# Reordered engine queues, an earlier coefficient load and shifted filter copies in a four-layer convolution kernel

## The chip, the cores and the metric

The kernel runs on one core of one Trainium2 chip. A core has TensorE (matmul, shown as PE, its weight loads as PEld), VectorE (DVE), ScalarE (ACT), GpSimd (POOL) and SyncE (SP), the last used here only to issue transfers, and 16 DMA engines. The metric is the device time of one execution in microseconds (us).

## The reference

The input x has 8 images of 64 channels of 256 x 256 float32. Four layers follow each other:

```python
# layer 0: attention over channels
att = einsum('bcn,bdn->bcd', q, q); att = softmax(max(att) - att)
x = gamma * einsum('bcd,bdn->bcn', att, q) + x
# layers 1 and 3: a separable long convolution per channel, k = hx (x) hy, causal in both axes
y = irfft2(rfft2(x, s=512) * rfft2(k, s=512) / 512, s=512)[..., :256, :256] + x * bias
# layer 2: shrinkage between a 2-D Haar transform and its inverse, two terms
f1 = haar2d(x)
for i in range(2):
    f4 = einsum('bchw,oc->bohw', f1 * v[i], conv_w[i])
    acc += sign(f4) * relu(abs(f4) - tau[i])
x = haar2d(acc, inverse=True) + x
```

hx and hy come from a small network of sines; they are computed once, at the start.

## The kernel before

Convolutions are done as products with Toeplitz matrices (`toeplitz`, four matmuls of 256 and 128 columns), the Haar transforms as products with sign matrices (`haar_fwd`, `haar_halves`, `haar_inv`). A Toeplitz matrix is never stored: a table of 128 partitions x 256 columns holds, in partition p, the filter from element p on, and it is loaded from `filt` in DRAM by `window` (line 228), which reads 128 overlapping rows of 1 KB, each one float further. Each (image, channel) plane needs two such tables (`tab_a`, `tab_b`, four buffers each) per convolution.

The work of the 8 images is software-pipelined in `timeline` (line 102). A forward stage `forward_stage(b, fwd, shrink, gram)` walks over 64 steps, four to a loop round (`quads`, line 68). In one step it does up to three things, for three different images of the batch: fwd is layer 1 and the forward Haar transform of one channel plane of image b+1, in five lagged parts (`on[0]` to `on[4]`); shrink is the middle of layer 2 for image b, 4 x 256 pixels of all channels per step, in halves a = 0 and 1; gram is a piece of layer 0's Gram matrix of image b+2. An inverse stage then does the inverse Haar transform and layer 3 of image b (inv) and layer 0's mixing of image b+2 (mix). There are one mixing-only start, one forward stage without shrinkage (b=-1), six forward stages with all three parts (b=0 to 5), one without Gram (b=6), one with shrinkage alone (b=7), and the inverse stages between them.

Every engine has its queue written out by hand, in program order, and waits on semaphores. The order inside one full step is, before the change:

- SP (line 288): wait for x1 and the second Toeplitz product of four planes back, load image (256 KB) and two tables (128 KB each); in odd j then wait for a turn (`c_copy`) and load 512 KB of coefficients, then 512 KB of pixels for the Gram.
- PE (line 486): first Toeplitz product of plane n (bank 0); product(0) of the shrinkage (line 498, bank 4); half a Gram piece; second Toeplitz product of plane n-1 (bank 1); product(1) (bank 5); the other half of the Gram piece; Haar (line 441); halves (line 457); turn (line 509), four transposes that wait for DVE's field of the step before.
- ACT (line 637): store of finished coefficients (line 659, an issue on its queue, waits for DVE's row repair); mid (664), the copy of bank 0; Abs(0) (643), Sign(0) (647), Relu(0) (652); Abs(1), Sign(1); high part of a plane (674); Relu(1); res (683).
- DVE (line 816): scale(0) (828), which reads product(0); two repairs of one row (843, 844); less(0) (835); field of the step before (853), which needs POOL's pair sums; scale(1); x1 (862); less(1); low part (869).
- POOL (line 932): for a = 0, 1 the multiplication by the sign (937) and the pair sum (940).

A product may overwrite its bank when the Relu of the same half of the step before is done (`c_relu`).

## Time and profile before

| | us |
|---|---|
| median of 3 runs | 7283.22 (7279.34 to 7286.21) |
| profiled execution | 7309.31 |
| its span | 7307.5 |
| PE busy in it | 6528.9 (89%) |
| PE weight loads | 5505.1 (75%) |
| DVE busy | 4081.2 (56%) |
| ACT busy | 3933.3 (54%) |
| POOL busy | 2583.9 (35%) |

The span runs from the first to the last instruction of the profiled execution; busy shares are averages over stages with different limits, so the stages are read one by one. A bracket behind an instruction says how long its engine stood idle before it and what ended that.

### The profile page before, as it was taken

The numbers are of one execution on the slowest core, as the hardware profiler recorded it, in microseconds if no ns is written. First come the engines' busy times: TensorE is split into PE (matmuls) and PEld (weight loads), VectorE is DVE, ScalarE is ACT, GpSimd is POOL, SyncE is SP. The second block draws the span as 40 slices with busy tenths as digits, with TensorE's granted clock in tenths as the row PEclk, the third lists the DMA queues.
The fourth block names the chain that finished last, engine by engine and source line by source line (L and its number), as shares of the span: only waits on it lengthen the run. The fifth ranks groups of instructions, "written<-read, shape, count | busy, mean of one in ns | idle before, by whom it ended". The sixth has DMA issues, their size and how long they took to land.

```text
span 7307.5 us, 143896 instructions
## 1 busy us (share of the span) xinstructions
PE 6528.9 (89%) x37984; PEld 5505.1 (75%) x37984; DVE 4081.2 (56%) x7293; ACT 3933.3 (54%) x7193; POOL 2583.9 (35%) x2564
## 2 busy tenths in 40 slices
PE   6896898999989999999999999899999988897679
PEld 4593787888878787787877888788887877686469
DVE  1241566556654566555664466645665466665556
ACT  1232565555655565555655566555655556655655
POOL 0000444224432344324442244423443244434642
PEclk9898999999999999999999999999999999999889
DMA  6786665876658666686667766586666855554136
GB/s 199 214 214 218 160 166 151 211 187 165 160 152 235 166 161 163 170 222 159 165 156 198 196 161 167 144 236 172 163 160 168 228 139 132 130 116 95 45 74 130
DMA packets 768925, 1214.59 MB, mean 166 GB/s; under 512 B 78742, under 2 KB 473143, under 8 KB 768664
## 3 DMA queue, kind: packets, MB, share of 16 engines
q1 hardware_dynamic: 621208, 942.99, 55.0%
q10 hardware_dynamic: 147456, 268.50, 9.6%
q8 instruction: 117, 1.92, 0.1%
q14 instruction: 144, 1.18, 0.1%
HBM read 808.13 MB, written 403.05 MB: 166 GB/s over the span
## 4 chain that ended last, share of the span: by engine, by line
PE 52%; DVE 11%; DMA 11%; issue 9%; ACT 8%; ACTq 3%; POOL 2%; SPq 2%; DVEq 1%; POOLq 0%
PE ps L431 17%; PE ps L433 9%; PE ps L449 7%; PE ps L498 6%; DMA rows<-coef 5%; PE ps L575 5%; PE ps L457 4%; DVE held L828 4%; ACT ps L643 3%; DMA mixed<-x 3%; DVE field L853 3%; ACT sgn L647 3%; PE ps L509 3%; ACTq L659 2%; DVE res L844 2%
## 5 line engine op out<-in xcount | busy, mean ns | idle before, releaser
L937 POOL TENSOR_TENSOR mag<-mag,sgn 128x512 f32<-128x512 f32 x1024 | 1187.9, 1160 | 2774.9 <-ACT mag L652 2772.9
L952 POOL TENSOR_TENSOR split_a<-field,split_a 128x512 fp32r<-128x512 f32 x512 | 652.1, 1274 | 1810.7 <-ACT split_a L712 1810.7
L835 DVE TENSOR_TENSOR ps<-ps,tau_t 128x512 f32<-128x512 f32 x1024 | 716.5, 700 | 1009.4 <-ACT ps L643 966.5
L431 PE MATMUL ps<-tab_a,img 128*128 128x256 f32 x4096 | 1244.6, 386 | 27.1 <-issue 11.0
L431 PE MATMUL ps<-tab_b,mid 128*128 128x256 f32 x4096 | 1229.3, 382 | 1.6 <-DVE x L862 1.5
L828 DVE TENSOR_TENSOR held<-ps,v_t 128x512 f32<-128x512 f32 x1024 | 704.3, 688 | 409.3 <-PE ps L498 380.0
L664 ACT ACTIVATE mid<-ps 128x512 f32<-128x512 f32 x512 | 305.7, 597 | 1154.4 <-PE ps L433 931.3
L433 PEld LDWEIGHTS ps<-tab_a,img 128*128 128x128 f32 x4096 | 785.1, 192 | 109.2
L433 PEld LDWEIGHTS ps<-tab_b,mid 128*128 128x128 f32 x4096 | 781.7, 191 | 106.7
L643 ACT ACTIVATE ps<-held 128x512 f32<-128x512 f32 x1024 | 613.8, 599 | 426.8 <-DVE held L828 426.8
L433 PE MATMUL ps<-tab_a,img 128*128 128x128 f32 x4096 | 792.2, 275 | 0.0
L433 PE MATMUL ps<-tab_b,mid 128*128 128x128 f32 x4096 | 789.8, 275 | 0.0
L940 POOL TENSOR_TENSOR pair_sum<-mag 128x256 f32<-128x256 f32 x1024 | 743.9, 727 | 121.9 <-POOL mag L937 81.2
L449 PE MATMUL ps<-s_inv,split_a 128*128 128x256 f32 x4096 | 701.7, 315 | 72.3 <-POOL split_a L952 39.1
L431 PEld LDWEIGHTS ps<-tab_a,img 128*128 128x128 f32 x4096 | 669.0, 193 | 102.9 <-issue 51.9
L449 PEld LDWEIGHTS ps<-s_inv,split_a 128*128 128x128 f32 x4096 | 551.0, 194 | 227.9 <-issue 213.3
L652 ACT ACTIVATE mag<-ps 128x512 f32<-128x512 f32 x1024 | 607.4, 593 | 177.9 <-DVE ps L835 177.9
L409 PEld LDWEIGHTS ps<-pix 128*128 128x128 f32 x4096 | 592.6, 192 | 89.9 <-DMA pix<-in_x_pix 48.8
L409 PE MATMUL ps<-pix 128*128 128x128 f32 x4096 | 613.9, 277 | 42.0 <-DMA pix<-in_x_pix 42.0
L431 PEld LDWEIGHTS ps<-tab_b,mid 128*128 128x128 f32 x4096 | 629.4, 193 | 6.2 <-DVE x L862 2.1
L700 ACT ACTIVATE x<-ps 128x512 f32<-128x512 f32 x512 | 306.2, 598 | 606.9 <-DMA mixed<-x 330.2
L647 ACT ACTIVATE sgn<-held 128x512 bf16<-128x512 f32 x1024 | 630.8, 616 | 0.0
(74 smaller groups left out, 10026.9 us busy)
## 6 DMA issues: line engine op xcount, KB each, us to landing
pix<-in_x_pix SPq DMA_DIRECT2D x256, 512.0 KB, 7.0
mixed<-x ACTq DMA_DIRECT2D x512, 256.0 KB, 5.3
img<-mixed SPq DMA_DIRECT2D x512, 256.0 KB, 2.8
tab_a<-filt SPq DMA_DIRECT2D x1024, 128.0 KB, 3.7
tab_b<-filt SPq DMA_DIRECT2D x1024, 128.0 KB, 4.7
coef<-res ACTq DMA_DIRECT2D x512, 256.0 KB, 3.9
out<-res SPq DMA_DIRECT2D x512, 256.0 KB, 4.8
pix<-in_x_rows SPq DMA_DIRECT2D x128, 512.0 KB, 6.0
```

The source lines that it names most:

```text
L409: mm = nc.tensor.matmul(ps[:, 7, 0:2 * C], pix[:, buf, j, :], pix[:, buf, j, :], start=False, stop=False, skip_group_check=True)
L431: nc.tensor.matmul(o_ps, src[:, 0, H * half:H * half + H], tab[:, N - 1::-1], start=True, stop=False)
L433: mm = nc.tensor.matmul(o_ps[:, H:N], src[:, 1, H * half:H * half + H], tab[:, N - 1:H - 1:-1], start=False, stop=True)
L449: mm = nc.tensor.matmul(ps[:, bank, N * half:N * half + N], src[:, piece, kh, H * half:H * half + H], s_inv[:, kh, :], start=(kh == 0 and ...
L643: nc.scalar.activation(ps[:, 4 + a, :], held[:, a], ACT.Abs).then_inc(c_abs, 1)
L647: nc.scalar.activation(sgn[:, a], held[:, a], ACT.Sign).then_inc(c_sign, 1)
L652: nc.scalar.activation(mag[:, a], ps[:, 4 + a, :], ACT.Relu).then_inc(c_relu, 1)
L828: nc.vector.tensor_tensor(held[:, a].rearrange(grouped, i=2, h=4), ps[:, 4 + a, :].rearrange(grouped, i=2, h=4), table(v_t, a), ALU.mult)\
L835: nc.vector.tensor_tensor(bank, bank, table(tau_t, a), ALU.subtract).then_inc(c_less, 1)
L937: nc.gpsimd.tensor_tensor(mag[:, a], mag[:, a], sgn[:, a], ALU.mult).then_inc(c_mult, 1)
L940: nc.gpsimd.tensor_tensor(pair_sum[:, a], mag[:, a, 0:N], mag[:, a, N:2 * N], ALU.add)\
L952: nc.gpsimd.tensor_tensor(split_a[:, 1], src, split_a[:, 0].bitcast(F32), ALU.subtract)\
```

## The change

It changes the order of the queues in the forward stages, and the way in which the filters lie in DRAM:

- PE: product(0), first Toeplitz product, product(1), half Gram, second Toeplitz product, half Gram, and the rest as before. The wait of the first step for the last result of the inverse stage (`i_res`) goes with product(0) to the front.
- ACT: mid; Abs(0), Sign(0), Abs(1), Sign(1), Relu(0); the store of coefficients; high part; Relu(1); res.
- DVE: scale(0); row repairs; scale(1); less(0); field; less(1); x1; low part.
- SP: in odd j the wait for the turn and the load of coefficients stand ahead of the wait for x1 and of the loads of image and tables. The load of pixels stays behind them.
- `filt` holds eight copies of each filter, copy s starting s floats further, with a pitch of 376 floats (1504 bytes). Eight stores write them. `window` reads partition 8a+s from copy s at offset 8a; each read still is 128 rows of 1 KB.

```diff
--- before.py
+++ after.py
@@ -33,6 +33,8 @@
 EMB = 33
 ORDER = 64
 QROW = N + H
+SHIFTS = 8
+SROW = QROW - SHIFTS
 CR = 5
 ROWS = 4
 CHUNKS = N // (2 * ROWS)
@@ -125,7 +127,7 @@
         def sem(name):
             return ctx.enter_context(nc.semaphore(name))
 
-        filt = nc.dram_tensor("filt", (4, C, QROW), F32, kind="Internal").ap()
+        filt = nc.dram_tensor("filt", (4, C, SHIFTS, SROW), F32, kind="Internal").ap()
         coef = nc.dram_tensor("coef", (B, C, H, 2 * N), F32, kind="Internal").ap()
         mixed = nc.dram_tensor("mixed", (C, H, 2 * N), F32, kind="Internal").ap()
 
@@ -227,8 +229,8 @@
 
         def window(f, c):
 
-            row = filt[f, bass.ds(c, 1), :]
-            return bass.AP(row.tensor, row.offset, [[1, H], [1, N]])
+            row = filt[f, bass.ds(c, 1), :, :]
+            return bass.AP(row.tensor, row.offset, [[SHIFTS, H // SHIFTS], [SROW, SHIFTS], [1, N]])
 
 
         @block.sync
@@ -278,7 +280,9 @@
                     load_pix(0, 2 * jj + buf, buf)
             sp.wait_ge(dve_init, 100)
             sp.nop(nofuse=True)
-            sp.dma_start(filt.rearrange("f c n -> c f n"), f_out).then_inc(filters_out, 16)
+            for s in range(SHIFTS):
+                sp.dma_start(filt[:, :, s, :].rearrange("f c n -> c f n"), f_out[:, :, s:s + SROW])\
+                    .then_inc(filters_out, 16)
 
             def forward_stage(b, fwd, shrink, gram):
                 if gram:
@@ -287,6 +291,10 @@
 
                 def step(q, j, on):
                     n = 64 * (b + 1) + 4 * q + j
+                    if shrink and j % 2 and not (isinstance(q, int) and q == 0):
+                        sp.wait_ge(c_copy, 64 * b + 4 * q + j - 3 + CR)
+                        sp.nop(nofuse=True)
+                        load_coef(b, 2 * q + j // 2, j // 2)
                     if fwd and not (isinstance(q, int) and q == 0):
                         sp.wait_ge(f_x1, n - 3 + CR)
                         sp.nop(nofuse=True)
@@ -295,10 +303,6 @@
                         load_img(4 * q + j, j)
                         fwd_tables(4 * q + j, j)
                     if j % 2 and not (isinstance(q, int) and q == 0):
-                        if shrink:
-                            sp.wait_ge(c_copy, 64 * b + 4 * q + j - 3 + CR)
-                            sp.nop(nofuse=True)
-                            load_coef(b, 2 * q + j // 2, j // 2)
                         if gram:
                             load_pix(b + 2, 2 * q + j // 2, j // 2)
                 quads(sp, 16, 0, step)
@@ -371,7 +375,7 @@
                         sp.wait_ge(s, 16 * (32 * (b + 2) + 32) + 16)
                         sp.nop(nofuse=True)
                     if b == -2:
-                        sp.wait_ge(filters_out, 16)
+                        sp.wait_ge(filters_out, 16 * SHIFTS)
                         sp.nop(nofuse=True)
                     else:
                         sp.wait_ge(f_mm2, 64 + CR)
@@ -516,16 +520,18 @@
                         if e % 2 and second:
                             mm.then_inc(gram_chunk, 1)
 
+                    if shrink and on[0]:
+                        if isinstance(q, int) and q == 0 and j == 0:
+                            pe.wait_ge(i_res, 64 * b + CR)
+                            pe.nop(nofuse=True)
+                        product(0)
                     if fwd and on[0]:
                         pe.wait_ge(img_in[j], 16 * (16 * (b + 1) + q) + 16)
                         pe.wait_ge(ftab_in[j], 32 * (16 * (b + 1) + q) + 32)
                         pe.wait_ge(f_mid, n + CR)
                         toeplitz(0, img[:, j], tab_a[:, j]).then_inc(f_mm1, 1)
                     if shrink and on[0]:
-                        if isinstance(q, int) and q == 0 and j == 0:
-                            pe.wait_ge(i_res, 64 * b + CR)
-                            pe.nop(nofuse=True)
-                        product(0)
+                        product(1)
                     if gram and on[1]:
                         gram_half(0)
                     if fwd and on[1]:
@@ -533,8 +539,6 @@
                         pe.wait_ge(f_mid, n + CR)
                         pe.wait_ge(f_x1, n - 1 + CR)
                         toeplitz(1, mid[:, d1 % 2], tab_b[:, d1 % 4]).then_inc(f_mm2, 1)
-                    if shrink and on[0]:
-                        product(1)
                     if gram and on[1]:
                         gram_half(1)
                     if fwd and on[2]:
@@ -651,6 +655,16 @@
                         act.wait_ge(c_pair, u + a - 1 + CR)
                         nc.scalar.activation(mag[:, a], ps[:, 4 + a, :], ACT.Relu).then_inc(c_relu, 1)
 
+                    if fwd and on[0]:
+                        act.wait_ge(f_mm1, n + 1 + CR)
+                        act.wait_ge(f_mm2, n - 1 + CR)
+                        nc.scalar.activation(mid[:, j % 2], halved(ps[:, 0, :]), ACT.Copy).then_inc(f_mid, 1)
+                    if shrink and on[0]:
+                        absolute(0)
+                        sign(0)
+                        absolute(1)
+                        sign(1)
+                        relu(0)
                     if fwd and on[4]:
                         d = j - 4
                         act.wait_ge(f_res, n - 4 + 1 + CR)
@@ -658,16 +672,6 @@
                         dst = coef[bass.ds(b + 1, 1), bass.ds(4 * q + d, 1), :, :].rearrange("b o p n -> p (b o n)")
                         act.dma_start(dst, res[:, d % 2].rearrange("p a n -> p (a n)"))\
                             .then_inc(coef_out[d % 2], 16)
-                    if fwd and on[0]:
-                        act.wait_ge(f_mm1, n + 1 + CR)
-                        act.wait_ge(f_mm2, n - 1 + CR)
-                        nc.scalar.activation(mid[:, j % 2], halved(ps[:, 0, :]), ACT.Copy).then_inc(f_mid, 1)
-                    if shrink and on[0]:
-                        absolute(0)
-                        sign(0)
-                        relu(0)
-                        absolute(1)
-                        sign(1)
                     if fwd and on[2]:
                         act.wait_ge(f_mm3, n - 1 + CR)
                         act.wait_ge(f_mm4, n - 2 + CR)
@@ -843,6 +847,7 @@
                         nc.vector.tensor_tensor(mean, mean, ps[0:1, 3, N:2 * N], ALU.add)
                         nc.vector.tensor_tensor(detail, ps[0:1, 3, 0:N], detail, ALU.subtract).then_inc(f_res, 1)
                     if shrink and on[0]:
+                        scale(1)
                         less(0)
                     if shrink and on[1]:
                         d = j - 1
@@ -854,7 +859,7 @@
                                                 ps[:, 6, :].rearrange("p (a c h) -> p a c h", a=2, h=4),
                                                 ALU.add).then_inc(c_field, 1)
                     if shrink and on[0]:
-                        scale(1)
+                        less(1)
                     if fwd and on[1]:
                         d = j - 1
                         dve.wait_ge(f_mm2, n + CR)
@@ -862,8 +867,6 @@
                         nc.vector.scalar_tensor_tensor(out=x1[:, d % 2], in0=img[:, d % 4],
                                                        scalar=bias1[:, bass.ds(4 * q + d, 1)], in1=halved(ps[:, 1, :]),
                                                        op0=ALU.mult, op1=ALU.add).then_inc(f_x1, 1)
-                    if shrink and on[0]:
-                        less(1)
                     if fwd and on[2]:
                         dve.wait_ge(f_hi, n - 1 + CR)
                         nc.vector.tensor_tensor(split_b[:, 1], halved(ps[:, 2, :]), split_b[:, 0].bitcast(F32),
```

## Rows read from the trace of the kernel before

**Rows 1.** Equal stretches: PE, PEld, DVE, ACT, POOL busy (x count), clock, DMA share, GB/s.
```profile
340.00:580.00 240.00, 240.00 (x1679) 225.57 (x1678) 103.51 (x199) 82.49 (x147) 0.00 (x0) 1.00 0.80 208
2480.00:2960.00 480.00, 443.99 (x2758) 386.54 (x2757) 314.51 (x536) 288.07 (x537) 226.47 (x240) 1.00 0.64 162
5920.00:6380.00 460.00, 377.76 (x2236) 324.72 (x2235) 309.94 (x529) 285.33 (x531) 220.86 (x235) 1.00 0.53 133
6690.00:7020.00 330.00, 202.38 (x693) 133.90 (x693) 189.79 (x288) 200.25 (x345) 216.67 (x231) 0.81 0.17 48
2130.00:2430.00 300.00, 297.30 (x1662) 246.07 (x1662) 154.20 (x306) 166.36 (x304) 76.23 (x60) 0.99 0.78 204
```

**Rows 2.** Line 509 in stages b=2, 6, 7: duration ns, first to last start.
```profile
L509 PE MATMUL ps<-eye,split_a x128: 272/273/330, 2461.5 to 2954.8; 128*128 128x128 f32 x128
...
L509 PE MATMUL ps<-eye,rows x128: 272/273/330, 2481.0 to 2970.6; 128*128 128x128 f32 x128
...
L509 PE MATMUL ps<-eye,split_a x128: 272/273/330, 5897.1 to 6369.7; 128*128 128x128 f32 x128
...
L509 PE MATMUL ps<-eye,rows x128: 271/273/330, 5909.0 to 6385.2; 128*128 128x128 f32 x128
...
L509 PE MATMUL ps<-eye,split_a x128: 272/328/477, 6669.2 to 7019.4; 128*128 128x128 f32 x128
...
L509 PE MATMUL ps<-eye,rows x128: 272/330/477, 6681.3 to 7031.0; 128*128 128x128 f32 x128
```

**Rows 3.** Line 441 in the forward-only stage, the same view.
```profile
L441 PEld LDWEIGHTS ps<-s_fwd,x x400: 188/192/192, 341.7 to 579.9; 128*128 128x128 f32 x134
```

**Rows 4.** Timeline of one step, PE alone: start, duration, what.
```profile
2607.91 0.66 PE L509 MATMUL ps<-eye,rows 128*128 128x128 f32 x4 [0.51 <-DVE field L853]
...
2608.40 0.60 PE L431 MATMUL ps<-tab_a,img 128*128 128x256 f32 x2
...
2609.71 1.03 PE L498 MATMUL ps<-chan_w,rows 128*128 128x256 f32 x4
...
2610.57 0.61 PE L409 MATMUL ps<-pix 128*128 128x128 f32 x4
...
2611.02 0.60 PE L431 MATMUL ps<-tab_b,mid 128*128 128x256 f32 x2
...
2614.45 0.71 PE L457 MATMUL ps<-split_b,s_fwd_half 128*128 128x512 f32 x2
...
2615.66 0.66 PE L509 MATMUL ps<-eye,rows 128*128 128x128 f32 x4 [0.49 <-DVE field L853]
```

**Rows 5.** Timeline of the same step, DVE and ACT.
```profile
2610.97 0.69 DVE L828 TENSOR_TENSOR held<-ps,v_t 128x512 f32<-128x512 f32 x1
...
2611.58 0.40 DVE L843 TENSOR_TENSOR res<-res,ps 1x256 f32<-1x256 f32 x1
...
2611.90 0.41 DVE L844 TENSOR_TENSOR res<-ps,res 1x256 f32<-1x256 f32 x1
...
2612.59 0.34 ACTq L659 DMA_DIRECT2D coef<-res  x1
...
2613.60 0.60 ACT L643 ACTIVATE ps<-held 128x512 f32<-128x512 f32 x1
...
2614.92 0.68 DVE L853 TENSOR_TENSOR field<-pair_sum,ps 128x512 f32 x1
```

**Rows 6.** Timeline of a late coefficient load.
```profile
2627.08 0.33 SPq L266 DMA_DIRECT2D rows<-coef  x1
...
2633.90 1.13 PE L498 MATMUL ps<-chan_w,rows 128*128 128x256 f32 x4 [0.34 <-DMA rows<-coef]
```

**Rows 7.** DMA issues in an inverse part (2130 to 2430): KB, median us to landing.
```profile
tab_b<-filt SPq DMA_DIRECT2D x57, 128.0 KB, 5.1
```

**Rows 8.** The page: a costly group, and the filter store among the DMA issues.
```profile
L937 POOL TENSOR_TENSOR mag<-mag,sgn 128x512 f32<-128x512 f32 x1024 | 1187.9, 1160 | 2774.9 <-ACT mag L652 2772.9
...
filt<-field SPq DMA_DIRECT2D x1, 384.0 KB, 4.6
```

## The prediction

> **What bounds the kernel now.** I read four views. First the busy times in equal stretches, one per kind of stage. They show that TensorE is the busiest engine everywhere, but not equally: in the forward part without shrinkage (340 to 580 us) it is busy for all of 240.0 us, in an inverse part 297.3 of 300 us, in shrinkage with forward part and Gram 444.0 of 480 us, without Gram 377.8 of 460 us, and in shrinkage alone 202.4 of 330 us [rows 1]. So the stages that the diff touches are the ones in which TensorE waits.
>
> Second, the turns of line 509, one group of four per step, which give the length of a step. The 64 steps of stage b=2 run from 2461.5 to 2970.6 us: 8.07 us a step. The six stages with Gram lie at 7.96 to 8.07, mean 8.03; the one without Gram takes 487.7/63 = 7.74, shrinkage alone 361.4/63 = 5.73 [rows 2].
>
> Third, the timeline of TensorE over one step: from 2608.40 (first Toeplitz product) to 2614.45 everything is back to back, then TensorE stands for 0.49 us until the turn at 2615.66, and the row says for whom: DVE's field of line 853 [rows 4]. Turn to turn this step is 7.75 us.
>
> Fourth, the other engines in that step [rows 5]: product(0) starts at 2609.71 only because the first Toeplitz product stands ahead of it; scale(0) follows at 2610.97, the two row repairs at 2611.58 and 2611.90, ACT's store of the coefficients (queued ahead of mid, and waiting for that repair) at 2612.59, then mid, Abs at 2613.60, less(0), field at 2614.92, turn, and again the Toeplitz product. That ring closes in 7.75 us. It is latency through four engines, no engine's own work. On top of it every other step is longer: the coefficient load is issued at 2627.08, behind an image and two tables, and product(0) starts at 2633.90, released by that DMA [rows 6]. The mean of 8.03 over the ring's 7.75 is this lateness, 0.28 us a step.
>
> **The change part by part.** *TensorE's own need per step.* The nearest proof of what it can do back to back is the forward-only stage: 50 steps, 8 loads each, from 341.7 to 579.9 us, so about (238.2 - 0.8)/49 = 4.85 us for two Toeplitz products, Gram, Haar and halves, with no wait [rows 1, 3]. Two products cost 0.86 each (2609.71 to 2610.57) and the turn 0.49 (2607.91 to 2608.40) [rows 4], counted as 0.45 when the next work is already there. Floor: 4.85 + 1.72 + 0.45 = 7.02, taken as 7.05. Nothing is removed from TensorE; the change can give at most the 0.98 us between 8.03 and 7.05.
>
> *Does the new order reach the floor?* I lay one step out, TensorE without waits, product(0) at 0: Toeplitz 0.86, product(1) 2.17, Gram 3.03, Toeplitz 3.48, Gram 4.79, Haar 5.24, halves 6.1, turn 6.55, next product(0) 7.0. A product is read 1.26 us after its start (2609.71 to 2610.97), and successors on one engine start 0.5 (ACT) and 0.6 us (DVE) apart [rows 4, 5]. DVE: scale(0) 1.26, repairs 1.86 and 2.2, scale(1) 3.43, less(0) 4.03, field 4.64, less(1) 5.25, x1 5.9, low part 7.7, done 8.4. ACT: mid 2.6, Abs 3.1, Sign 3.6, Abs 4.15, Sign 4.7, Relu(0) 5.2, store 5.8 to 6.5, high part 7.0 (it needs the halves of the image before, 6.1 + 0.9), Relu(1) 7.5, res 8.0, done 8.6. POOL, from Relu(0)'s end at 5.8: multiply 1.16 [rows 8] and pair sum about 0.75, then those of Relu(1) from 8.2 to about 10.2. Each of TensorE's waits then has room: the next product(0), at 7.0, needs Relu(0), done at 5.8; product(1), at 9.2, needs Relu(1), 8.1; the next turn, at 13.55, needs field, 12.3, which needs the pair sums of 10.2 and starts at 11.6. The least room is 1.0 us. ACT's store, until now in the ring, hides behind these; if that cover went, its 0.7 us would delay Relu(1), which has 1.0. The next thing late is TensorE itself.
>
> *Coefficients asked for earlier.* On SP's queue the load of step (q, j) is now ahead of that step's wait for x1 and of its image and two tables, so it goes out right behind the former trio, one step (7 us) and 2 us of issues sooner. Its own wait (turn of step 4q+j-4) is then already met, so nothing is queued behind it for long; the image and tables behind it have buffers four deep and about 15 us of room. Needed 12 us after its issue where 6.8 us pass in [rows 6], the 0.28 goes. With the new engine order but the old place it would be late by about 1 us in every second step. The pixel load of the Gram stays behind the tables.
>
> *Stages with Gram:* 0.98 x 63 x 6 = 370 us. *Without Gram:* the floor is less by the two Gram halves, 0.45 each (2610.57 to 2611.02 [rows 4]), 6.15; the same layout leaves ACT 0.5 us and the turn 0.3 us of room, I take 6.25: (7.74 - 6.25) x 63 = 94 us. *Shrinkage alone:* here POOL's two multiplies and pair sums, Relu(1) and the next product(1) form a ring over two steps, some 9.9 us; I take 5.1: 0.63 x 63 = 40 us, with ends 0 and 60, since the granted clock is 0.81 there [rows 1], part of the time on the 1.2 GHz level.
>
> *What it costs.* At each entry the first Toeplitz product now stands behind product(0) and its waits for i_res and the coefficients: no row shows this order; between 0 and two products on the 1.2 GHz level (3.4 us) each, I take 1.5 x 7 = 10 us. The filter store becomes eight: 384 KB landed in 4.6 us [rows 8]; eight such, 37 us if serial, 5 if only the issues count, and the first x_rows loads stand behind them on the same queue; I take 10 us, once.
>
> *Tables in copies.* Same bytes, same 128 rows of 1 KB, another address pattern in HBM. In an inverse stage tab_b lands in 5.1 us [rows 7] and TensorE is busy 99% [rows 1], so a faster table is hidden: 0 to -3 us a stage, I take -10 in all. DMA share is 0.64 in the stages with Gram; in 7.05 instead of 8.0 us a step it becomes about 0.73, and the forward-only stage ran at 0.80 without one wait of TensorE [rows 1].
>
> The rows thus say that a 1 KB table row is cheap to hide whatever its start. The Trainium skill ("DMA: Bandwidth & Descriptors", How a descriptor splits into AXI transactions) speaks against this part: a transaction must start at a 256 B boundary, and bytes in front of an unaligned start are fetched for nothing. Copies shifted by eight floats start on multiples of 32 B, not 256 B, so by that rule (an estimate from it) nearly every row still splits in five; the tables' part of the sum would be 0 instead of -10. No row here separates the two.
>
> *Sum* against the profiled execution, 7309.3 us (span 7307.5): 370 + 94 + 40 + 10 - 10 - 10 = 494, so 6815. The median of the runs shown, 7283.2, is 0.36% below the profiled one; the same share off 6815 gives 6790, forecast 6790.
>
> **The rivals.** *A second ring stays.* If something that I placed with little room is later (high part behind the halves, then Relu(1), POOL, field), a step takes 7.4 instead of 7.05, likewise without Gram: +0.35 x 63 x 7 = 154, so 6945. For it: six of ACT's nine activations are now in a row. Against it: room of 1.0 us and more. Chance 0.15.
>
> *TensorE's floor is lower than the pieces say.* Weight loads are busy 386.5 of 480 us, 81% [rows 1], 6.46 us a step. If a step could shrink to that: 0.59 x 63 x 6 = 223 more, 6570. Against it: the stage that has no wait shows 225.6 of 240 us, 94%, not 100% [rows 1]. Chance 0.04. Beside this the Trainium skill ("Perfetto Trace Analysis", Identifying the Most-Contended Engine) says that the busy share of weight loads, not of matmuls, tells TensorE's headroom.
>
> *Slower: the eight copies are read more slowly.* Place: the inverse stages, where a table is asked for once the product of four images back is done and is needed some two steps (about 10 us) later. Landing in 5.1 us it is hidden; from about 11 us on TensorE waits in each of 512 steps, and at 13 us a step grows by about 1.3: +665, so 7455. For it: the 1504-byte pitch between copies is shown nowhere. Against it: the traffic is the same and the rows are spread over more addresses. It outweighs the gain only beyond a landing of some 12 us. Chance 0.05.
>
> *The change doesn't do what it says:* the turn's wait moves to product(0) (Relu(0) late by over 1.2 us) and the step stays at 7.75; only the coefficient part and small things are left. With the lateness gone too this is 6 x 63 x 0.28 = 106, 7180; with it put back, no change, 7283. Together 0.08, of which 0.03 within the bound.
>
> **How the numbers follow.** Forecast 0.68, its own range 6700 to 6890 (unknowns: filter store 5 to 37, entries 0 to 24, shrinkage alone 0 to 60, a step 6.95 to 7.2). The range 6690 to 6960 takes in the second ring, 0.83 in all. About 0.2% (15 us) is what a measurement of this kernel can tell from none. Faster: 0.68 + 0.15 + 0.04 + 0.05 = 0.92; same 0.03; slower 0.05.
>
> **What would show it.** Turn to turn 7.0 to 7.1 us with Gram and no idle time before line 509; about 6.2 without Gram and 5.1 in shrinkage alone; product(0) never released by a coefficient DMA, its load issued some 12 us ahead; tab_b landing at or under 5 us; mixing starting up to 10 us later than now. I am wrong if an idle time of over 0.2 us a step stands ahead of a product or the turn, or if the inverse stages are longer.

## The result and the profile after

The changed kernel takes 6846.85 us (median of 4 runs, 6837.41 to 6851.19) where the kernel before takes 7281.28: a ratio of 0.9401, 95% interval 0.9385 to 0.9417. Forecast were 6790 and 6690 to 6960. The profiled execution has a span of 6843.3 us against 7307.5, 464 us less; the medians differ by 434. The profiled execution of the kernel before, 7309.31 us, lies outside the 7278.04 to 7286.21 us of its runs here and inside the 7302 to 7315 us that it took on two other chips in the experiments. So it was probably taken on such a chip, and some 28 of the 464 us are probably the chip's.

The first view is that of equal stretches (start:end and length, then busy us of PE, PEld, DVE, ACT, POOL, clock, DMA share, GB/s): a stage with all three parts, the one without Gram, and shrinkage alone.

```profile
1560.00:1980.00 420.00, 420.00 (x2747) 387.63 (x2747) 308.33 (x537) 288.83 (x538) 224.61 (x239) 1.00 0.58 184
5520.00:5880.00 360.00, 360.00 (x2229) 328.15 (x2228) 302.04 (x527) 283.04 (x527) 219.55 (x235) 1.00 0.54 170
6200.00:6550.00 350.00, 225.99 (x689) 161.90 (x689) 182.30 (x287) 192.07 (x345) 212.11 (x229) 0.67 0.14 45
```

Where [rows 1] had PE waiting, with Gram it is now busy for 420.00 of 420 us and without Gram for 360.00 of 360. The DMA share, 0.64 before, is 0.58 in shorter steps, not the 0.73 that I expected; without the copies (e1 below, the same stretch) it is 0.69. Shrinkage alone went the other way: the granted clock is 0.67 in place of 0.81.

The turns (line 509, now 513) of stages b=2, 6 and 7 answer to [rows 2].

```profile
L513 PE MATMUL ps<-eye,split_a x128: 270/272/331, 2334.9 to 2766.8; 128*128 128x128 f32 x128
...
L513 PE MATMUL ps<-eye,rows x128: 270/272/273, 2351.3 to 2780.9; 128*128 128x128 f32 x128
...
L513 PE MATMUL ps<-eye,split_a x128: 270/272/328, 5506.5 to 5883.2; 128*128 128x128 f32 x128
...
L513 PE MATMUL ps<-eye,rows x128: 270/272/273, 5520.3 to 5895.4; 128*128 128x128 f32 x128
...
L513 PE MATMUL ps<-eye,split_a x128: 272/421/477, 6180.6 to 6555.9; 128*128 128x128 f32 x128
...
L513 PE MATMUL ps<-eye,rows x128: 272/273/477, 6194.0 to 6567.8; 128*128 128x128 f32 x128
```

With Gram from 2334.9 to 2780.9, 7.08 us a step in place of 8.07; without Gram 6.17 in place of 7.74; shrinkage alone 6.13 in place of 5.73. From first to last turn (the starts of each turn's first transpose) the sums against the span are:

| part | before | after | gained | forecast |
|---|---|---|---|---|
| six stages with Gram | 3035.2 | 2672.4 | 362.8 | 370 |
| stage without Gram | 487.7 | 388.6 | 99.1 | 94 |
| shrinkage alone | 361.1 | 386.5 | -25.4 | +40 |
| six gaps between stages, with mixing | 2113.9 | 2086.5 | 27.4 | 10, less 10 for the entries |
| up to the first turn | 747.9 | 747.7 | 0.2 | -10 |
| the gap ahead of b=7, the end | 561.6 | 561.7 | -0.1 | 0 |

One step with Gram, in the timeline of PE, DVE and ACT, against [rows 4] and [rows 5]:

```profile
1706.93 1.03 PE L502 MATMUL ps<-chan_w,split_a 128*128 128x256 f32 x4
...
1708.21 0.69 DVE L832 TENSOR_TENSOR held<-ps,v_t 128x512 f32<-128x512 f32 x1
...
1709.10 1.03 PE L502 MATMUL ps<-chan_w,split_a 128*128 128x256 f32 x4
...
1710.47 0.69 DVE L832 TENSOR_TENSOR held<-ps,v_t 128x512 f32<-128x512 f32 x1 [0.92 <-PE ps L502]
...
1711.67 0.68 DVE L858 TENSOR_TENSOR field<-pair_sum,ps 128x512 f32 x1
...
1712.14 0.34 ACTq L673 DMA_DIRECT2D coef<-res  x1
...
1713.53 0.60 PE L513 MATMUL ps<-eye,split_a 128*128 128x128 f32 x4
```

Product(0) starts at 1706.93, product(1) at 1709.10, turn at 1713.53, with no bracket on PE: nothing is waited for. Scale(0) follows product(0) by 1.28 us, the store of line 673 goes out at 1712.14, about 3 us after the repairs, and no turn or product waits for it. Counted from product(0), scale(1) comes at 3.54 and field at 4.74 us; laid out by hand they were at 3.43 and 4.64.

The coefficients' load and the product that uses them, against [rows 6]:

```profile
1708.95 0.34 SPq L268 DMA_DIRECT2D rows<-coef  x1
...
1721.00 1.03 PE L502 MATMUL ps<-chan_w,rows 128*128 128x256 f32 x4
```

12 us ahead, as forecast.

### The profile page after: what moved, and what is told of

Its sections match the earlier page's. It is cut to its first block, busy times and chain, and to the rows that moved or that the text cites. A ratio compares the mean times of both kernels' runs of the same rounds, so it can differ in the third digit from the quotient of the medians.

```text
span 6843.3 us, 143405 instructions
## 1 busy us (share of the span) xinstructions
PE 6388.8 (93%) x37984; PEld 5552.1 (81%) x37984; DVE 4030.1 (59%) x7293; ACT 3928.3 (57%) x7193; POOL 2576.2 (38%) x2564
## 4 chain that ended last, share of the span: by engine, by line
PE 88%; DMA 4%; issue 2%; DVE 2%; ACT 1%; POOL 1%; SPq 1%; ACTq 0%; DVEq 0%; POOLq 0%
PE ps L435 26%; PE ps L502 13%; PE ps L437 13%; PE ps L453 7%; PE ps L461 7%; PE ps L445 7%; PE ps L413 6%; PE ps L579 5%; PE ps L513 3%; DMA mixed<-x 3%; POOL mag L940 1%; DMA pix<-in_x_pix 1%; ACT x L704 1%; DVE field L858 0%; DVE held L832 0%
## 5 line engine op out<-in xcount | busy, mean ns | idle before, releaser
L437 PEld LDWEIGHTS ps<-tab_a,img 128*128 128x128 f32 x4096 | 787.5, 192 | 110.3
L435 PEld LDWEIGHTS ps<-tab_a,img 128*128 128x128 f32 x4096 | 707.6, 193 | 82.4 <-issue 6.6
L678 ACT ACTIVATE split_b<-ps 128x512 fp32r<-128x512 f32 x512 | 305.7, 597 | 608.8 <-PE ps L461 600.8
L716 ACT ACTIVATE split_a<-field 128x512 fp32r (+1 forms) x512 | 322.7, 630 | 545.1 <-PE ps L453 451.0
```

The lines of the kernel that those rows point to most:

```text
L435: nc.tensor.matmul(o_ps, src[:, 0, H * half:H * half + H], tab[:, N - 1::-1], start=True, stop=False)
L437: mm = nc.tensor.matmul(o_ps[:, H:N], src[:, 1, H * half:H * half + H], tab[:, N - 1:H - 1:-1], start=False, stop=True)
```

## The experiments

Ratios are to the kernel before, run on the same chip in the same rounds; the intervals are about 0.0016 wide to each side. The other columns are us from each profile: a step is the mean between turns, the gap is from the last turn of a stage with Gram to the first of the next (six of them, all with mixing). The chips differ: the kernel before took 7281 us on the chip of the result and on that of e3 to e6, and 7308 us on that of e1, e2, e7 and e8 and on that of e9 to e12. The changed kernel was not run on the last two. From e7, e8 and e9 with the difference of their last stage taken back (24, 61 and 30 us) it would take about 6850 us there, an estimate, and its ratio there would be about 0.937 in place of 0.9401. So ratios of different chips compare only to about 0.003; smaller differences are read from the steps and from runs on one chip.

| kernel | ratio | step with Gram | without | alone | gap |
|---|---|---|---|---|---|
| before | 1 | 8.03 | 7.74 | 5.73 | 352.3 |
| changed | 0.9401 | 7.07 | 6.17 | 6.13 | 347.8 |
| e3 copies alone | 0.9912 | 7.86 | 7.74 | 5.74 | 348.3 |
| e4 early coefficients alone | 0.9929 | 7.88 | 7.74 | 5.73 | 352.4 |
| e6 early coefficients, PE's order | 0.9754 | 7.54 | 7.47 | 5.74 | 353.7 |
| e5 early coefficients, ACT's store moved | 0.9380 | 7.08 | 6.15 | 5.73 | 350.6 |
| e11 ACT's store moved alone | 0.9393 | 7.12 | 6.28 | 5.73 | 350.9 |
| e10 changed, store at the front | 0.9425 | 7.07 | 6.71 | 6.14 | 348.6 |
| e1 changed, without copies | 0.9393 | 7.07 | 6.17 | 6.15 | 352.3 |
| e2 changed, coefficients late | 0.9415 | 7.06 | 6.62 | 6.18 | 347.5 |
| e7 changed, old last stage | 0.9335 | 7.06 | 6.20 | 5.76 | 347.5 |
| e8 changed, useless matmuls in the last stage | 0.9291 | 7.07 | 6.19 | 5.17 | 347.9 |
| e9 both e7 and e8 | 0.9332 | 7.06 | 6.17 | 5.66 | 347.6 |
| e12 e5 with copies and useless matmuls | 0.9333 | 7.07 | 6.15 | 5.64 | 346.9 |

### The ring: which of the three orders mattered

**e5_store_moved.** The kernel before with SP's coefficient load as in the change, and on ACT:

```diff
-                    if fwd and on[4]:
...
-                        act.dma_start(dst, res[:, d % 2].rearrange("p a n -> p (a n)"))\
-                            .then_inc(coef_out[d % 2], 16)
                     if fwd and on[0]:
...
                     if shrink and on[0]:
                         absolute(0)
                         sign(0)
                         relu(0)
+                    if fwd and on[4]:
...
+                        act.dma_start(dst, res[:, d % 2].rearrange("p a n -> p (a n)"))\
+                            .then_inc(coef_out[d % 2], 16)
+                    if shrink and on[0]:
                         absolute(1)
                         sign(1)
```

> The kernel before with the early coefficient load and ACT's store moved from the front of its step to behind Relu(0); the orders of TensorE and DVE and ACT's other work stay as before. Theory: the ring of 7.75 us goes through the store only because mid and Abs(0) are queued behind it; without it the ring is first Toeplitz product, product(0), scale(0), Abs, less, field, turn, about 5.9 us, below TensorE's 7.04: turn to turn 7.04, without Gram 6.14, shrinkage alone 5.73 as before; 7281 - 459, about 6822. Rival: the gain needs all three orders together, then a step is 7.3 us or more and the time 6920 or more.

Measured: ratio 0.9380, 6828.64 us. Its turns in stage b=2 (same columns as above):

```profile
L509 PE MATMUL ps<-eye,split_a x128: 270/272/273, 2326.7 to 2756.7; 128*128 128x128 f32 x128
...
L509 PE MATMUL ps<-eye,rows x128: 270/272/273, 2341.2 to 2770.7; 128*128 128x128 f32 x128
```

7.05 us a step, with PE's and DVE's orders untouched. One transfer's issue, moved by four places in one queue, gives the whole gain of the steps. The rival that all three orders are needed is out.

**e11_store_only.** The same move alone, coefficients in their old place:

> The kernel before with ACT's store moved behind Relu(0), the coefficient load in its old place and the filters stored once. Theory: the rings are below 7.04, but the coefficients, landing in 6.5 us, are asked for too late and every second step is about 1 us longer: mean 7.5 us, 7281 - 6 x 63 x 0.5 (with Gram) - 100 (without), ratio about 0.96. Rival: the load has enough lead, 7.04, ratio 0.938 as with the early load.

Measured: 7.12 us a step and a ratio of 0.9393, not 0.96. The early load is worth 0.04 us a step with Gram and 0.13 without, once the ring is open. My mean lateness of 0.5 us a step was wrong: the load does go out late, but it mostly just arrives.

**e6_pe_order.** The kernel before with the early coefficient load and PE's new order alone:

```diff
+                    if shrink and on[0]:
...
+                        product(0)
                     if fwd and on[0]:
...
                         toeplitz(0, img[:, j], tab_a[:, j]).then_inc(f_mm1, 1)
                     if shrink and on[0]:
...
-                        product(0)
+                        product(1)
                     if gram and on[1]:
                         gram_half(0)
                     if fwd and on[1]:
...
                         toeplitz(1, mid[:, d1 % 2], tab_b[:, d1 % 4]).then_inc(f_mm2, 1)
-                    if shrink and on[0]:
-                        product(1)
```

> The kernel before with the early coefficient load and TensorE's new order alone (product(0) first, product(1) behind the first Toeplitz product). Theory: the ring loses the 1.31 us of the Toeplitz product, 6.4 us, below 7.04: TensorE bound with Gram, 7.04; without Gram the ring's 6.4 shows instead of 6.14: 7281 - 459 + 16, about 6838. Rival: mid, which waits for that Toeplitz product, keeps it in the ring, and the step stays at 7.3 to 7.75: 7000 to 7175.

Measured: 7.54 us a step. The rival's number came, but not by its mechanism. The timeline of DVE and ACT over one period shows a ring that has no TensorE work in it:

```profile
1802.77 0.68 DVE L828 TENSOR_TENSOR held<-ps,v_t 128x512 f32<-128x512 f32 x1
...
1803.48 0.60 ACT L643 ACTIVATE ps<-held 128x512 f32<-128x512 f32 x1 [0.59 <-DVE held L828]
...
1804.54 0.58 ACT L674 ACTIVATE split_b<-ps 128x512 fp32r<-128x512 f32 x1
...
1805.15 0.69 DVE L869 TENSOR_TENSOR split_b<-ps,split_b 128x512 fp32r<-128x512 f32 x1 [0.24 <-ACT split_b L674]
...
1805.76 0.68 DVE L828 TENSOR_TENSOR held<-ps,v_t 128x512 f32<-128x512 f32 x1
...
1806.68 0.41 DVE L844 TENSOR_TENSOR res<-ps,res 1x256 f32<-1x256 f32 x1
...
1807.37 0.34 ACTq L659 DMA_DIRECT2D coef<-res  x1
...
1807.90 0.60 ACT L664 ACTIVATE mid<-ps 128x512 f32<-128x512 f32 x1 [1.81 <-DVE res L844]
...
1808.39 0.60 ACT L643 ACTIVATE ps<-held 128x512 f32<-128x512 f32 x1
...
1809.11 0.70 DVE L835 TENSOR_TENSOR ps<-ps,tau_t 128x512 f32<-128x512 f32 x1 [2.02 <-ACT ps L643]
...
1809.72 0.68 DVE L853 TENSOR_TENSOR field<-pair_sum,ps 128x512 f32 x1
...
1810.31 0.68 DVE L828 TENSOR_TENSOR held<-ps,v_t 128x512 f32<-128x512 f32 x1
```

Scale(1), Abs(1), (Sign(1)), high part, low part, scale(0), repair, store, mid, Abs(0), less(0), field and scale(1) again: 1802.77 to 1810.31, 7.54 us, each starting at most 0.72 us after the one before it. The products that scale(0) and scale(1) read had started over 2 us earlier, so TensorE is not in it. In the kernel before, this second ring lay just under the first one of 7.75. The store stands in both, which is why moving it opens both and moving product(0) opens only one. Mid, at 1807.90, follows the store's issue by 0.53 us, so it waits for ACT's own queue and not for PE.

**e10_store_front.** The changed kernel with the store back in front:

```diff
+                    if fwd and on[4]:
...
+                        act.dma_start(dst, res[:, d % 2].rearrange("p a n -> p (a n)"))\
+                            .then_inc(coef_out[d % 2], 16)
                     if fwd and on[0]:
...
                     if shrink and on[0]:
...
                         relu(0)
-                    if fwd and on[4]:
...
-                        act.dma_start(dst, res[:, d % 2].rearrange("p a n -> p (a n)"))\
-                            .then_inc(coef_out[d % 2], 16)
```

> The changed kernel with ACT's store of coefficients back at the front of ACT's step, all other orders as changed. Theory: in the kernel before a ring of DVE and ACT alone (scale(0), repairs, store, mid, Abs, Sign, high part, low part, scale(0)) closed in 7.53 us; with the Abs, Sign and Relu of the new order it is about 6.4 us: turn to turn 7.04 with Gram, 6.4 without (6.14 with the store behind Relu(0)), so +16 us on the changed kernel, ratio 0.942. Rival: the store's place is what decides, with it in front a step is 7.3 to 7.5 us, ratio 0.955 to 0.97.

Measured: 0.9425; 7.07 with Gram as forecast, but 6.71 without. So with Gram the other orders, with the early coefficients and the copies, also reach TensorE's bound without the store's move, and the ring with the store in it is 6.7, 0.3 more than I laid out. The rival (0.955 to 0.97) is out.

### The coefficients and the copies

**e4_coef_only.** The kernel before with the SP part of the change alone.

> The kernel before with the coefficient load alone moved ahead on SP's queue. Theory: lateness gone, ring stays: 7.75 us in every step, 7281 - 106 = 7175, inverse parts as before. Rival: the coefficient transfer now collides with the tables and delays them, less than 50 us gained.

**e3_copies_only.** The kernel before with the eight copies alone.

> The kernel before with the eight copies alone. Theory: the engine ring stays at 7.75 us, but the coefficients land in about 3.8 instead of 6.5 us and are no longer late, so steps lose their 0.28 us (106 us), and the inverse parts 4.5 us each: 7281 - 106 - 27, about 7150. Rival (the copies only move bytes that are hidden): 7270 to 7290.

Measured: e4 0.9929 (7234.46 us), e3 0.9912 (7220.86 us). Both gain less than half of what I gave them. The steps go from 8.03 to 7.88 and 7.86, not to 7.75. The timeline of PE in e4, stage b=2, at the start of a round of four steps (the turn before it, first Toeplitz product, product(0), next turn):

```profile
2642.51 0.66 PE L509 MATMUL ps<-eye,rows 128*128 128x128 f32 x4 [0.49 <-DVE field L853]
...
2643.28 0.69 PE L431 MATMUL ps<-tab_a,img 128*128 128x256 f32 x2
...
2644.68 1.03 PE L498 MATMUL ps<-chan_w,split_a 128*128 128x256 f32 x4
...
2650.68 0.66 PE L509 MATMUL ps<-eye,split_a 128*128 128x128 f32 x4 [0.54 <-DVE field L853]
```

From turn to turn 8.17 us, though the coefficients are there. The first Toeplitz product starts 0.77 us after the turn, where it is 0.49 in [rows 4], and product(0) 1.40 us after that, where it is 1.31. This comes once in four steps, at the loop's round, so 0.10 of the 0.28 us that I had put down to late coefficients was the round's. In the changed kernel it is gone by itself: there PE never stands at that point.

**e1_no_copies.** The changed kernel with the filters stored once and read in overlapping rows.

> The changed kernel with the filters stored once and read as overlapping rows again; all else as changed. Theory: the copies halve the landing times (tables 4 to 5 us to 2.7, coefficients 6.5 to 3.7), but with the coefficients asked for 12 us ahead this hides; turn to turn stays at 7.04 us. Only the inverse parts with mixing (347.8 us from turn to turn after, 352.3 before) take their 4.5 us each back, and the start gives back some of its eight stores: 6843 + 27 - 8, about 6865. Rival: the landing times carry part of the 7.04, then steps become uneven, 7.1 to 7.4, and the time 6900 to 7000.

**e2_late_coef.** The changed kernel with SP's order as before:

```diff
-                    if shrink and j % 2 and not (isinstance(q, int) and q == 0):
...
-                        load_coef(b, 2 * q + j // 2, j // 2)
                     if fwd and not (isinstance(q, int) and q == 0):
...
                         load_img(4 * q + j, j)
                         fwd_tables(4 * q + j, j)
                     if j % 2 and not (isinstance(q, int) and q == 0):
+                        if shrink:
...
+                            load_coef(b, 2 * q + j // 2, j // 2)
```

> The changed kernel with the coefficient load back behind image and tables on SP's queue. Theory: issued 5 us ahead of its product instead of 12, and landing in 3.7 us thanks to the copies, it is just in time: turn to turn 7.04, time 6847, no change. Rival, as the prediction had it: late by about 1 us in every second step, +0.5 x 63 x 7 = 220 us, 7070.

Measured: e1 0.9393 and 6868.74 us, e2 0.9415. In e1 the steps do not move and each gap takes back 4.5 us, as forecast. That 6868.74 lies so near the 6865 expected is in part luck, since the 6865 was reckoned from another chip; and the ratio, no higher than the 0.9401 of the changed kernel, shows no loss for the same reason. Against the 6850 us estimated for this chip e1 is about 19 us longer, where 18 were forecast. Landing times (KB each, median us) in a stage with Gram, of the changed kernel:

```profile
tab_b<-filt SPq DMA_DIRECT2D x61, 128.0 KB, 2.6
rows<-coef SPq DMA_DIRECT2D x15, 512.0 KB, 3.8
```

and of e1:

```profile
tab_b<-filt SPq DMA_DIRECT2D x61, 128.0 KB, 4.5
...
rows<-coef SPq DMA_DIRECT2D x15, 512.0 KB, 4.9
```

The kernel before has 6.5 us for the coefficients in that stage (6.8 up to the product in [rows 6]). The fall has two reasons: 4.9 is reached without the copies, 3.8 with them (3.7 in e7, on e1's chip). That the rest is the new place is shown by e11 and e5, which differ in it alone: 6.3 and 4.9 us over the whole run. I had expected the copies to give all of it. For tab_b in an inverse part they do: 5.1 us in [rows 7] and in e1, 2.9 in the changed kernel. In e2 with Gram nothing is lost, 7.06; without Gram, where a step is 6.14 at best, the load comes too late and a step takes 6.62. The prediction's 1 us in every second step holds there and nowhere else.

The copies are paid for at the start. SP's queue in the changed kernel

```profile
110.14 13.81 SPq L284 DMA_DIRECT2D filt<-field  x8
124.04 3.88 SPq L258 DMA_DIRECT2D pix<-in_x_rows  x2
```

and in the kernel before

```profile
115.67 0.83 SPq L256 DMA_DIRECT2D pix<-in_x_rows  x2
```

The eight stores hold it for 13.81 us, and the first x_rows load goes out at 124.04 instead of 115.67. The first turn, equal in the profiles before and after (probably of different chips), is at 749.9 us in e3 and at 734.6 to 736.9 in e4, e5 and e6, which ran on the same chip: about 14 us, where I took 10. Six gaps of 4.5 us less this leaves the copies some 13 us, under what the ratios can tell.

### The last forward stage

**e7_tail_old.** The changed kernel with the old order of DVE and ACT where `fwd` is false:

```diff
                         absolute(0)
                         sign(0)
+                        if not fwd:
+                            relu(0)
                         absolute(1)
                         sign(1)
-                        relu(0)
+                        if fwd:
+                            relu(0)
```
```diff
                     if shrink and on[0]:
-                        scale(1)
+                        if fwd:
+                            scale(1)
                         less(0)
...
                     if shrink and on[0]:
+                        if not fwd:
+                            scale(1)
                         less(1)
```

> The changed kernel, but the last forward stage (shrinkage alone) has the old order of DVE and ACT. Theory: its turn waits for a field that now stands behind scale(1), so two products lie in the ring instead of one; with the old order turn to turn goes from 6.13 back to 5.73 us: -25 us, 6822. Rival: that stage is slower for another reason (loads, SP), then nothing changes.

Measured: 0.9335, a step of 5.76 and 6824.61 us. The stage's clock:

```profile
6195.00:6545.00 350.00, 219.35 (x734) 144.50 (x734) 200.75 (x305) 212.56 (x367) 228.26 (x244) 0.79 0.17 48
```

0.79 in place of 0.67. Why the new order is longer there shows in the changed kernel's timeline, one period from field to field:

```profile
6387.60 0.68 DVE L858 TENSOR_TENSOR field<-pair_sum,ps 128x512 f32 x1
...
6388.33 0.66 PE L513 MATMUL ps<-eye,rows 128*128 128x128 f32 x4 [2.17 <-DVE field L858]
...
6388.82 3.45 PE L502 MATMUL ps<-chan_w,rows 128*128 128x256 f32 x8
...
6390.80 0.69 DVE L832 TENSOR_TENSOR held<-ps,v_t 128x512 f32<-128x512 f32 x1 [1.91 <-PE ps L502]
...
6392.51 0.69 DVE L832 TENSOR_TENSOR held<-ps,v_t 128x512 f32<-128x512 f32 x1 [1.01 <-PE ps L502]
6393.11 0.69 DVE L839 TENSOR_TENSOR ps<-ps,tau_t 128x512 f32<-128x512 f32 x1
...
6393.71 0.68 DVE L858 TENSOR_TENSOR field<-pair_sum,ps 128x512 f32 x1
```

Field to turn 0.73, turn to product(0) 0.49, product(0) to scale(0) 1.98, to scale(1) 1.71, less(0) 0.60, field 0.60: 6.11 us. With Gram at a clock of 1.00 product(0) to scale(0) is 1.28 us, and a product takes 0.86. Here the two products take 3.45 us together, twice as much, as at the 1.2 GHz level, and two of them lie in the ring where before there was one. With 1.28 and 0.86 in place of 1.98 and 1.71 the ring would be 4.56 us, an estimate.

**e8_tail_filler.** The changed kernel with eight matmuls of zeros into the bank that the Gram leaves free, ahead of each turn of that stage:

```diff
+                    def warm(count):
+                        for _ in range(count if not fwd else 0):
+                            nc.tensor.matmul(ps[:, 7, 0:2 * C], zero[:, :], zero[:, :], start=True, stop=True)
...
+                    warm(8)
                     if shrink and on[0]:
                         turn()
```

> The changed kernel with eight matmuls without use (zeros into a free bank) ahead of each turn of the last forward stage, where TensorE idles about 2.2 us. Theory: that stage is longer than the 5.1 us predicted because TensorE is granted 0.67 of its clock there and both products and the turn lie in the ring; busy, it is granted 1.0 and a step takes 4.6 to 5.2 us, -60 to -95 us, so 6750 to 6790. Rival: the clock does not matter, the ring is that long at any clock, and the fillers (1.7 us at 2.4 GHz, 3.4 at 1.2 GHz) lie in the idle time or lengthen it: 6.1 us or more, 6847 or above.

Measured: 0.9291 (0.9276 to 0.9307), 6790.76 us. The stage's stretch and its turns:

```profile
6200.00:6510.00 310.00, 258.55 (x1684) 226.67 (x1683) 196.37 (x301) 196.38 (x361) 224.02 (x241) 1.00 0.19 54
...
L513 PE MATMUL ps<-eye,split_a x128: 272/273/330, 6193.8 to 6509.5; 128*128 128x128 f32 x128
...
L513 PE MATMUL ps<-eye,rows x128: 272/273/330, 6204.1 to 6519.6; 128*128 128x128 f32 x128
```

Clock 1.00 and 5.17 us a step, 0.96 us less than without the useless work. The order was not slow; the clock was. What keeps the step at 5.17, above the 4.56 estimated for the ring, is not taken apart. What lowered the clock in the new order is shown only so far: in a stretch of 350 us PE waited 125.8 us ahead of 58 turns, 2.17 us each; before, in 330 us, it was 97.8 us ahead of 58 turns, 1.69 each, and 29.6 us ahead of products. This is also the fastest of all these kernels; of its 0.011 in ratio against the changed one its stage accounts for 61 us, 0.008, and the rest is within what the chips differ.

**e9_tail_old_filler** puts both together (four such matmuls behind product(0), not ahead of it as the expectation has it, and five ahead of the turn), **e12_least** is e5 with the copies and the same matmuls, the four here ahead of product(0).

> The changed kernel; in the last forward stage the old order of DVE and ACT, and matmuls without use (four ahead of product(0), five ahead of the turn). Theory: one product in the ring and the clock at 2.4 GHz: 4.6 to 5.0 us a step in place of 6.13, ratio 0.924 to 0.928. Rival: with the old order TensorE's share of the ring is small, the clock gives little, 5.4 us, ratio 0.931 to 0.933.

> The kernel before with the eight copies, the early coefficient load, ACT's store behind Relu(0) and the same useless matmuls in the last forward stage; the orders of TensorE and DVE are not touched. Theory: that is all the change needs: steps of 7.04, 6.14 and 4.6 to 5.0 us, as in the changed kernel with the old last stage and the same matmuls, ratio within 0.002 of it. Rival: with the tighter room of the old orders stalls show beside the copies, 0.005 or more above it.

Measured: 0.9332 and 0.9333, steps of 5.66 and 5.64 at a clock of 0.98 in e9. The old order in this stage takes 5.6 to 5.8 us at either clock, so my 4.6 to 5.0 was wrong and the rival nearer. The timeline of e9 shows why: its ring has no TensorE work in it, so no clock shortens it.

```profile
6401.19 1.16 POOL L952 TENSOR_TENSOR mag<-mag,sgn 128x512 f32<-128x512 f32 x1 [1.66 <-ACT mag L662]
...
6403.39 0.69 DVE L868 TENSOR_TENSOR field<-pair_sum,ps 128x512 f32 x1 [0.86 <-POOL pair_sum L955]
6403.99 0.68 DVE L841 TENSOR_TENSOR held<-ps,v_t 128x512 f32<-128x512 f32 x1
...
6404.71 0.60 ACT L653 ACTIVATE ps<-held 128x512 f32<-128x512 f32 x1 [1.55 <-DVE held L841]
...
6406.16 0.60 ACT L662 ACTIVATE mag<-ps 128x512 f32<-128x512 f32 x1 [0.30 <-DVE ps L848]
...
6406.84 1.15 POOL L952 TENSOR_TENSOR mag<-mag,sgn 128x512 f32<-128x512 f32 x1 [1.56 <-ACT mag L662]
```

POOL's multiplication, its pair sum, field, scale(1), Abs(1), less(1), Relu(1) and the multiplication again close in 5.65 us: in the old order scale(1) stands behind field. With the new order scale(1) stands ahead of it, and the clock decides, 6.13 or 5.17. And e12, with PE's and DVE's orders untouched, is equal to e9: in the stages with Gram and the one without, the rest of the reordering brings nothing that the store's move doesn't. It pays only in the last stage, and only with the clock held (e8).

## Why the prediction was right, and where it was off

*TensorE's floor.* 7.05 was taken, 7.04 came as the median step (mean 7.07 with the slower first steps); without Gram 6.25 was taken and 6.14 came. The sum of pieces from a stage that has no wait was good to 0.02 us. The Trainium skill ("Perfetto Trace Analysis", Identifying the Most-Contended Engine) judges TensorE's headroom by the rate of its arithmetic and by the busy share of weight loads. That share is 387.63 of 420 us, 92%, at this bound; a floor of 6.46 us did not come.

*The ring.* That a ring of 7.75 us through four engines, and not PE, set the step was right, and the experiments show it. Right was also that the store stood in it. Unseen was the second ring of 7.54 us on DVE and ACT alone; with it I would have known that moving product(0) is not enough and moving the store is.

*Coefficients.* The lead of 12 us came. The step that failed is to put all of 8.03 - 7.75 down to them: 0.15 us of it was theirs by e4's step (0.12 by its time, 46 us in 378 steps), 0.10 the loop's round. As both went, the sum was not hurt.

*Shrinkage alone.* This is the term that was mis-sized: +40 forecast, -25 came. Of the 57 us between 6790 and 6847 it is 65; the other terms gave 35 back. The remaining 27 are the step from the profiled execution to the median: I took 0.36% off, as before, but the changed kernel's profiled execution, 6845.18 us, lies at its median and not above it. The 0.36% was probably the difference of two chips and not of a profiled execution. The step 5.1 us was a layout at 2.4 GHz, and e8 with the clock held there gives 5.17. What failed is the bound: I had the granted clock of 0.81 in [rows 1], took it for a widening of 0 to 60, and did not ask whether the new order makes the ring depend more on the clock. The new order put a second product into the ring, and the idle time before each turn rose from 1.69 to 2.17 us; the clock fell to 0.67.

*Costs.* Filter store 10 taken, about 14 came (e3 against e4 to e6; the table's 0.2 hides it, its profiles being probably of two chips). The entries' 10 us are not visible: the six gaps fell by 4.6 us each, all of which e1 gives back. So the tables' -10 was too small, -27 came. By the rule of the Trainium skill ("DMA: Bandwidth & Descriptors", How a descriptor splits into AXI transactions) the copies should gain nothing, an estimate. The runs say otherwise: tab_b lands in 2.6 us with copies and in 4.5 without (e1). Whether that comes from starts on multiples of 32 B or from 128 rows no longer lying over each other, no run separates.

*The rivals.* None of them came. The slower one (copies read more slowly) is out, they are read faster; a ring at 7.4 us is not there in the changed kernel, though one of 6.7 stood behind it (e10).

## What to carry to other kernels

When an engine with the most work still waits once in every step, write down the whole ring of starts that closes in one step, and then look for the next ring below it: an instruction that stands in both, even a transfer's issue that costs half a microsecond and whose own data nobody waits for, is the one to move. Price a stage in which TensorE idles at the granted clock of its rows, and ask how many matmuls the new ring holds. Lateness seen every second step and a loop's round every fourth look alike in a mean; read a few steps in a row.

## What the runs showed of the hardware

Eight useless matmuls per step took the granted clock of a stage with idle time from 0.67 to 1.00 and made it 16% shorter (6.13 to 5.17 us a step). Reading 128 rows of 1 KB that overlap by all but 4 bytes costs other transfers too: with eight shifted copies tab_b landed in 2.6 instead of 4.5 us and coefficient loads of 512 KB in 3.8 instead of 4.9 us, at the same bytes (e1 against the changed kernel). A loop's round lengthened the step by 0.4 us where PE waited at that point (e4, 8.17 against 7.77), and by nothing that shows where it had work queued (7.04 in each of the four steps of the changed kernel). In shrinkage alone with scale(1) behind field, a clock of 0.98 in place of 0.79 gave 0.1 us a step (5.76 in e7, 5.66 in e9); the ring there runs over POOL, DVE and ACT.
